# Last message layer and projections as one stage, with ScalarE evicting and biases added by products of ones

## The reference, cut to what matters

```
h = x
for _ in range(3):
    msgs = relu(h[src] @ W_edge + b_edge)
    agg  = segment_sum(msgs, dst, num_segments=50000)
    h    = relu(concatenate([agg, h], -1) @ W_agg + b_agg)
x1 = layernorm(x + h)                     # no gain, no bias, eps 1e-5
q, k, v, skip = (x1 @ W + b  for Wq, Wk, Wv, Wskip)
...                                       # attention over dst, feed-forward, two norms
```

## Time and profile before

| what | us |
|---|---|
| median of 3 runs | 6480.81 |
| lowest, highest | 6471.52, 6483.21 |
| the profiled execution | 6482.03 |
| its span | 6480.2 |
| PE busy | 4587.8 (71%) |
| DVE busy | 3774.3 (58%) |
| POOL busy | 3525.7 (54%) |
| ACT busy | 1885.8 (29%) |

### The profile page before, as it was taken

How to read it: one execution, slowest core, us unless ns; L and a number is a source line. 1 busy time by engine, 2 the same in 40 slices (tenths; PEclk the granted TensorE clock), 3 DMA queues, 4 the chain that set the end, 5 groups by cost and what they waited for, 6 DMA issues and landing times. The chain is left out here.

```text
span 6480.2 us, 105856 instructions
## 1 busy us (share of the span) xinstructions
PE 4587.8 (71%) x19910; PEld 2854.0 (44%) x19911; DVE 3774.3 (58%) x12450; ACT 1885.8 (29%) x4118; POOL 3525.7 (54%) x3741
## 2 busy tenths in 40 slices
PE   5666657777777777666666777466666666888887
PEld 3444445555555555444443333244444443333333
DVE  7666633333333333333347888577777776777777
ACT  0222223333333333011110000122222222666665
POOL 1555554444344443544434555666666653888887
PEclk9888878888878888777788999655555555999999
DMA  1333345545455454333336888433333332333333
GB/s 34 127 126 124 131 126 149 155 149 153 148 149 151 149 154 146 112 109 108 108 102 220 266 270 268 149 89 88 91 91 88 88 85 69 101 104 104 104 106 96
DMA packets 732213, 840.28 MB, mean 130 GB/s; under 512 B 150205, under 2 KB 575272, under 8 KB 732068
## 3 DMA queue, kind: packets, MB, share of 16 engines
q1 hardware_dynamic: 619172, 619.89, 29.9%
q0 software_dynamic: 112896, 218.94, 13.4%
HBM read 439.86 MB, written 398.61 MB: 129 GB/s over the span
## 5 line engine op out<-in xcount | busy, mean ns | idle before, releaser
L762 POOL DMA_INDIRECT mp_gathered<-msg_rows,other_idx x1176 | 1120.9, 953 | 1411.5 <-PE bank L781 902.1
L781 PE MATMUL bank<-mp_edge_hot,mp_gathered 128*128 128x256 bf16 x5292 | 933.6, 308 | 458.6 <-issue 400.7
L781 PEld LDWEIGHTS bank<-mp_edge_hot,mp_gathered 128*128 x5292 | 560.9, 106 | 743.6 <-issue 637.9
L840 ACT ACTIVATE mp_h_out<-bank,mp_b_agg 128x256 f32<-128x256 f32 x588 | 278.7, 474 | 1429.6 <-PE bank L799 749.3
L525 POOL DMA_INDIRECT by_window<-so_pay,so_pos_i x392 | 395.2, 1008 | 437.6 <-issue 305.5
L1206 POOL DMA_INDIRECT at_kv<-kv_rows,kv_idx x392 | 422.1, 1077 | 348.1 <-DVE at_v_e L1355 241.5
L874 DVE TENSOR_SCALAR mp_edge_hot<-digits,mp_first_col,column 128x256 bf16<-128x256 bf16 x1764 | 506.1, 349 | 109.6 <-issue 74.8
L799 PE MATMUL bank<-mp_h_in,mp_w_agg_h 128*128 128x256 f32 x1176 | 474.0, 491 | 109.1 <-issue 103.7
L897 DVE TENSOR_TENSOR mp_msg_out<-mp_rest,mp_msg_out 128x256 bf16<-128x256 f32 x392 | 166.3, 424 | 650.2 <-ACT mp_msg_out L853 393.2
L1490 POOL DMA_INDIRECT ff_agg<-at_rows,last_idx x392 | 414.1, 1056 | 96.7 <-issue 89.0
L1208 POOL DMA_INDIRECT at_q<-q_rows,node_idx x392 | 393.5, 1004 | 126.7 <-issue 126.7
(11 more groups left out here) (217 smaller groups left out, 9283.4 us busy)
## 6 DMA issues: line engine op xcount, KB each, us to landing
mp_h_in<-h_cols SPq DMA_DIRECT2D x588, 128.0 KB
h_cols<-mp_h_out SPq DMA_DIRECT2D x588, 128.0 KB
msg_rows<-mp_msg_out SPq DMA_DIRECT2D x392, 192.0 KB
kv_rows<-pn_proj SPq DMA_DIRECT2D x98, 512.0 KB
msg_rows<-so_msg_out SPq DMA_DIRECT2D x98, 384.0 KB
h_cols<-so_h_out SPq DMA_DIRECT2D x98, 256.0 KB
pn_h_in<-h_cols SPq DMA_DIRECT2D x98, 256.0 KB
x_rows<-pn_x_b SPq DMA_DIRECT2D x98, 256.0 KB
```

The source lines that it names most:

```text
L762: pool.indirect_dma_start(gathered[:, r * PARTS * D:(r + 1) * PARTS * D], None, core.msg_rows[layer % 2], bass.IndirectOffsetOnAxis(ap=cor ...
L781: product = nc.tensor.matmul(agg_bank[k], gathered[:, bass.ds(at + d * D, D)], hot, start=(first and d == 0), stop=True, skip_group_check= ...
```

## The change

`message_passing` keeps two layers (`range(LAYERS - 1)`) and loses the target counting. `project_nodes` is gone. A new stage `last_layer` does the third layer and the projections; it stands before `last_edges`. Its parts:

- The edge sums come out node by feature: the 0/1 matrix is now the weight and the gathered part is moved, so a block takes 3 tiles x 2 halves x 3 parts = 18 products of 128 columns. The h part likewise: the block's `h` columns are the weight, W_agg the moved part, one product per half. A group's four halves share one bank, begun by one product of ones (3 rows) with the bias split in three bf16 parts. h is no longer stored in `h_cols`, nor loaded and transposed by groups.
- DVE takes relu and adds x in one instruction, takes the moments, and makes 1/deviation in five small steps from a square root that ACT gives, with a shift for ACT. POOL only gathers.
- ACT normalises (four instructions), copies the transposed columns, and evicts all four projection tiles with a plain copy.
- Each projection tile is begun by a product of ones with the split biases; the identity is added to Wskip once, so that the skip part contains x1. DVE adds b2.
- The loop is written out for 8 blocks, with lags of up to 8 blocks; 0/1 matrices have 8 buffers instead of 4, target matrices 4 instead of 2; x, y and x1 have four.

The core of the diff:

```diff
-def project_nodes(core, x, w, b):
+def bias_parts(core, dve, chain, at, src, rest, hi, mid, parts):
+    nc = core.nc
+    nc.vector.tensor_copy(hi, src).then_inc(chain, 1)
+    dve.wait_ge(chain, at + 1)
+    nc.vector.tensor_tensor(rest, src, hi, ALU.subtract).then_inc(chain, 1)
+    nc.vector.tensor_scalar(parts, hi, core.ident[0:PARTS, 0:1], None, ALU.mult).then_inc(chain, 1)
...
+    return at + 7
+def last_layer(core, W_agg, b_agg, x, w, b):
+    rows_bank, x1_bank, proj_bank = bank[2:4], bank[0], [bank[1], bank[4], bank[5], bank[7]]
...
+            def store(g):
+                k = g % 2
+                reached(sp, xb2_ok, g + 1)
+                sp.dma_start(rows(core.x1_rows, g), x1_b2[k][:, :, :]).then_inc(st_x1[k], 16)
+                reached(sp, by_act, T * (g + 1))
+                sp.dma_start(rows(core.kv_rows, g), proj[k][:, :, 0:2 * D]).then_inc(st[k], 16)
+                sp.dma_start(rows(core.q_rows, g), proj[k][:, :, 2 * D:3 * D]).then_inc(st[k], 16)
+                sp.dma_start(rows(core.skip_rows, g), proj[k][:, :, 3 * D:4 * D]).then_inc(st[k], 16)
...
+            for n in range(NW + 10):
+                if n + RING - 1 < NW:
+                    reached(sp, block_mm, n)
+                    load_h(n + RING - 1)
+                if n % 2 == 0 and n // 2 + Q - 1 < NG:
+                    reached(sp, y_ok, n // 2)
+                    load_x(n // 2 + Q - 1)
+                if n % 2 and 0 <= n // 2 - 4 < NG:
+                    store(n // 2 - 4)
...
+            def add_tile(r, i, hot):
+                at = (i & (TILES - 1)) * (PARTS * D)
+                for half in range(2):
+                    to = rows_bank[r // 2 % 2][:, (r % 2 * 2 + half) * P:(r % 2 * 2 + half + 1) * P]
+                    for d in range(PARTS):
+                        product = nc.tensor.matmul(to, hot(half), gathered[:, bass.ds(at + d * D, D)], start=False, stop=True, skip_group_check=True)
+                return product
...
+            def project(g, q, j):
+                pe.wait_ge(cols_ok, g + 1)
+                for t in range(T):
+                    reached(pe, by_act, T * (g - 1) + t + 1)
+                    nc.tensor.matmul(proj_bank[t][:, :], core.ones[0:PARTS, :], proj_parts[:, :], start=True, stop=True, skip_group_check=True)
+                    nc.tensor.matmul(proj_bank[t][:, :], x1_cols[q % 2][:, t * P:(t + 1) * P], weights[:, :], start=False, stop=True,
+                                     skip_group_check=True).then_inc(mm, 1)
+            def turn(do):                       # PE
+                do(0, sum_edges)
+                do(0, count_targets)
+                do(-6, group(turn_x1))
+                do(-8, group(project))
...
+            def evict(g, q, j):
+                reached(act, st[q % 2], 48 * (2 * j + q // 2))
+                for t in range(T):
+                    act.wait_ge(mm, T * g + t + 1)
+                    nc.scalar.activation(proj[q % 2][:, t, :], proj_bank[t][:, :], ACT.Copy).then_inc(by_act, 1)
+            def turn(do):                       # ACT
+                do(0, group(roots))
+                do(-4, group(x1_columns))
+                do(-2, group(normalize))
+                do(-6, group(evict))
...
+            def add_rows(g, q, j):
+                dve.wait_ge(block_mm, 2 * g + 2)
+                dve.wait_ge(x_ld[q], 16 * (j + 1))
...
+                nc.vector.scalar_tensor_tensor(out=y[q][:, :, :], in0=rows_bank[q % 2][:, :].rearrange("p (t f) -> p t f", t=T), scalar=0.0,
+                                               in1=x_in[q][:, :, :], op0=ALU.max, op1=ALU.add).then_inc(y_ok, 1)
+                dve.wait_ge(y_ok, g + 1)
+                norm_stats(nc, dve, stat_c, g, y[q], stats[q], moments[q]).then_inc(mom_ok, 1)
...
+            def turn(do):                       # DVE
+                do(-3, group(add_rows))
+                do(-6, group(deviations))
+                do(-8, group(add_b2))
+                do(0, hots)
+                do(0, target_hots)
```

More of the change, by code:

```diff
@@ L741, in _ @@
                 told = [0] * (TILES // TOLD)
-                for layer in range(LAYERS):
+                for layer in range(LAYERS - 1):
                     if layer:
@@ L833, in _ @@
                 act.wait_ge(wts, 5 * 16)
[L834 to L835 removed]
+                for layer in range(LAYERS - 1):
+                    wins, turns_done = layer * NW, layer * (NW // RING)
                     def close_block(n, r, j):
@@ new lines, in last_layer, with rows, blocks, straight @@
+        x1_t, cols_ok, mm, by_act = (core.sem("ll_" + n) for n in (
+            "x1_transposed", "x1_cols_ready", "product", "proj_by_scalar"))
+        def rows(t, g):
+            return t[g * GR:(g + 1) * GR, :].rearrange("(p k) f -> p k f", k=T)
+        def blocks(eng, turn):
+            def straight(n):
+                def do(lag, step):
+                    if 0 <= n + lag < NW:
+                        step(n + lag, (n + lag) % TURN, (n + lag) // TURN)
+                turn(do)
+            for n in range(2 * TURN):
+                straight(n)
+            with aligned(eng, 2, NW // TURN) as j:
+                for r in range(TURN):
+                    turn(lambda lag, step: step(TURN * j + r + lag, (r + lag) % TURN, j + (r + lag) // TURN))
+            for n in range(NW // TURN * TURN, NW + 2 * TURN):
+                straight(n)
@@ new lines, in group, with at_second_block, edge_tiles @@
+        def group(step):
+            def at_second_block(n, r, j):
+                if r % 2:
+                    step(Q * j + r // 2, r // 2, j)
+            return at_second_block
+        words = {}
+        def edge_tiles(eng, n, r):
+            if r == 0:
+                words[eng.engine] = nc.values_load_multi_w_load_instructions(
+                    core.spans[0:1, bass.ds(n, TURN)], engines=[eng.engine], min_val=0, max_val=512 * NT - 1,
+                    skip_runtime_bounds_check_because="both halves are masked and only address tables of their size")[1]
+            word = words[eng.engine][r]
+            return word & 511, word >> 9
@@ L963, in project_nodes, with further @@
+        def further(eng, n, first, last, more):
+            with eng.If(first + (ALWAYS - 1) < last):
+                before = eng.value_load(core.more_before[0:1, bass.ds(n, 1)], min_val=0, max_val=NT - 1)
+                with eng.Fori(first + (ALWAYS - 1), last) as i:
+                    more(i, (before + i - (first + (ALWAYS - 1))) & 511)
         block = s.enter_context(nc.Block())
-        def rows(t, g):
-            return t[bass.ds(g * GR, GR), :].rearrange("(p k) f -> p k f", k=T)
@@ L1029, in turn, with roots @@
             def turn(do):
-                do(2, turn_h)
-                do(0, turn_x1)
-                do(-1, project)
-            turns(pe, turn)
+                do(0, sum_edges)
+                do(0, count_targets)
+                do(-6, group(turn_x1))
+                do(-8, group(project))
+            blocks(pe, turn)
         @block.scalar
         def _(act):
-            def x1_columns(g, k, i):
+            act.wait_ge(zero_ok, 2)
+            def roots(g, q, j):
+                act.wait_ge(mom_ok, g + 1)
+                reached(act, rstd_ok, g - Q + 1)
+                nc.scalar.activation(root[q][:, :], moments[q][:, :, 1], ACT.Sqrt, bias=eps_col[:, 0:1], scale=0.25).then_inc(root_ok, 1)
@@ new lines, in hot, with hots, more @@
+            def hot(to, n, i):
+                return nc.vector.tensor_scalar(to, core.digits[:, :], first_col[:, bass.ds(n, 1)], core.column[:, bass.ds(i, 1)],
+                                               ALU.add, ALU.is_equal)
+            def hots(n, r, j):
+                def more(i, at):
+                    dve.wait_ge(tile_mm, at + n + 1)
+                    hot(more_hot[:, bass.ds((at & 1) * W, W)], n, i + 1).then_inc(more_hot_ok, 1)
+                first, final = edge_tiles(dve, n, r)
+                reached(dve, block_mm, n - HOTS + 1)
+                for c in range(ALWAYS):
+                    made = hot(edge_hot[r % HOTS][:, c, :], n, first + c)
+                made.then_inc(edge_hot_ok, 1)
+                further(dve, n, first, final, more)
@@ L1114, in attention @@
+            blocks(dve, turn)
+            dve.wait_ge(dst_mm, NW)
+            nc.vector.tensor_copy(core.dst_count[0:NG, :], count_bank).then_inc(tabs_ok, 1)
 def attention(core, edge_attr, We):
```

329 lines of the change are left out of this document (174 added, 155 removed).

## The result

The kernel after takes 6204.39 us, the median of 4 runs (6200.82 to 6207.68), beside 6482.01 (6471.52 to 6491.08) for the kernel before in 4 runs. The ratio is 0.9572, with an interval of 0.9556 to 0.9589: 277 us less, where 122 were forecast and 6230 was the low end of the range. The direction was right and the size wrong.

The account below looks back on a forecast made before the run. PE's stream plus about 7 us per burst of gathers bounds the old layer. Start 20, 49 cycles of 28.0 us (1372), ends 12 and 11 make 1415 against 1537: 122 less, so 6359 us, range 6230 to 6560.

Parts of the forecast that it names:

- Array time per group, 10.0 us: PE in the new stage: products of a group of two blocks sum to 9.7 us, taken as 10.0 with idling.
- The 128-column edge products: PE's edge sums in the new stage: 36 products a group at 0.082 us each, 2.95 us (2.0 to 4.0).
- The ones: PE's new products of ones times bias parts: five a group, each twice 0.11 us, 1.1 us in all.
- Issue, 2.5 to 3.5 us a block: PE's instruction issue in the new stage: 2.5 to 3.5 us a block, 5 to 7 a group; the array ends last.
- Start 20, end 12 and 11: Around the new stage: 20 us before it, 12 for the last group's chain and stores, 11 for last edges and barrier.
- The burst, 8.0 us: PE's loss in each of 49 bursts of gathers in the new stage: 8.0 us, ends 3.7 and 12.
- the second rival: At PE's edge sums, a burst costs more with the longer stream: 12 us each, 196 us more, 6555; chance 0.25.
- The first rival: On PE, the stop hides under queued projections: loss 3.7 us a burst, 211 us less, 6150; chance 0.10.
- Rivals on the other side: New stage slower: dearer bursts, 6555, 0.25; PE loop code fetched again, 6498, 0.08; serial DVE/ACT/PE wait, 6460 to 6550, 0.07.

Follow-up runs that it names:

- Experiment 2: Kernel after, with the addresses of a tile's gathered parts worked out anew for the second half: 6459.93 us, ratio 0.9966.
- Experiment 1: Kernel after, with the long float32 product of each projection tile left out (x1 W not computed): 6022.45 us, ratio 0.930.
- experiment 6: Kernel after, with POOL gathering in bursts of four instead of eight (CHUNK 4) in all layers: 5940.48 us, ratio 0.9167.
- experiments 13 and 15: Kernel after, with gathers in fours and the projection's float32 product left out, run twice on chips without the stop: 5423.50 and 5408.43 us.

## Why the prediction was wrong

Direction and place held, and so did most terms. The step that failed is the price of a burst, which was carried over from the old layers without the cover that the new stream gives.

- *Array time per group, 10.0 us:* 10.2 by the rhythm of the blocks. The 128-column edge products came at the low end: 18 of them take 1.18 us, the last of them 0.22, so 0.96/17 = 0.056 us each, not 0.082. The Trainium skill's 81 ns for such a pair (TensorE: Matmul & The Clock Gate, "Back-to-back issue gap") is not what this trace shows. The ones were dearer than twice 0.11: 0.3 to 0.5 each. The two errors cancel by luck.
- *Issue, 2.5 to 3.5 us a block:* 1.9 undisturbed, since the addresses of the first half are used again (1809 register instructions of the main kind for 3528 products) and the projection lets PE's queue run ahead. Experiment 2 shows what it costs if they aren't: 256 us.
- *Start 20, end 12 and 11:* the first block ended 26 us after the layer before, and from the last block to attention it took 43 instead of 23: four projections of 5.7 us stand behind the last block, which the sum left out. Some 26 us too little.
- *The burst, 8.0 us:* this is the step that failed: "the loss per burst was 7.0", carried over and raised by one, with no overlap between the stop and the queued projection. A burst cost 4.1, 49 x 3.9 = 191 us less. Experiment 1 shows what made the difference: without the long products a burst costs the new stage 10 us and the pauses double (254 against 112 us). So without cover a burst costs this stage more than it cost the old layers, which is the second rival's direction, and some 6 of the 10 us lie under the transposes and the projection, which take 8.3 less 1.9 = 6.4 us of PE. With the 26 us above and 0.4 us more array time in each of 49 cycles, the three misses make -145 of the -153 us between 1415 and 1262.
- *The first rival* was this mechanism, at 3.7 us a burst and a chance of 0.10. Its mechanism is shown. Its price came near 4.1 by luck: it took 8.0 less 4.3, where the runs have 10 less 6. The argument that kept its chance low, that in the first layers 0.86 us more array work a block hid nothing, was misread: the last layer has the counts in place of part of it, so by busy time the first layers carry only (633.4 - 568.4)/196 = 0.33 us more a block, and none of it is a row of long products like the projection's 5.5 us.
- *Rivals on the other side:* no register instruction of the edge products took over 0.9 us, and a burst cost less than before, not more, as long as the projection covered it. The instruction queue moved 0.92 MB in the whole run, 0.93 in the kernel before, so nothing was brought again at the loop's returns. No wait between ACT, DVE and PE showed: PE's idle time is issue.

What a stop costs PE is not what its absence is worth. In the old layers PE lost the seven us to the stop and not to POOL: in layer one PE's waits for POOL are 8.3 us and its idle time put down to issue is 188, while POOL waits for PE 296.6 us, in 40 waits.

```profile
PE bank L781 <- issue: 134.2, 180, 6.3
PE bank L781 <- POOLq L748: 8.3, 4, 3.9
POOL mp_gathered L762 <- PE bank L781: 296.6, 40, 9.9
```

But without the stop the first two layers gain only 4.1 us a cycle, since POOL's own pace of 13.1 comes next, above PE's 10.0. In the new stage PE needs 20.4 a cycle, POOL's pace is hidden, and the whole 4.1 that a burst costs is gained. If the old last layer gains what the first two do, which no trace shows, that is why the change is worth 278 us with and without the stop. POOL's pace could have been read from the kernel before: a gather every 1.25 us and the landing of the last make 13 us for four blocks. I had looked at POOL's waits for PE alone.

What stays open is what in a burst holds PE's issue: the kind of the gather or more than four microseconds of POOL's descriptors without a break, and why some chips don't show it. Open too is whether fours hide the stop in the new stage by their length or by the cover. In the first layers, which have no long products, fours cost no more with the stop than without: 786 and 795 us from the first block to the last (experiment 6), and 805 to 812 in experiments 13 and 15.

## What to carry to other kernels

A stall's price belongs to the stream in which it was measured: before carrying it to another, look at what will stand queued when it begins, since long work runs on through it. A cycle less the pace of one engine is what a stall costs that engine, not what its removal is worth: for that, work out the pace of each engine that takes part, its waits for its own transfers among them, and take only what stands above the slowest. Work that is taken from an engine beside a stall may have been its cover (98 us taken, 66 given back). Here it paid to shorten the stall first and take the work away then: 95 of 98 us arrived. Moving work to an engine that has room can still fail by its place in that engine's order: two of four tiles gave 95 us, four gave nothing.

## What the runs showed of the hardware

- While POOL issues gathers without a break, PE's issue is held from about 4 us into the burst until about 2 us behind the last one (experiment 1). Products with fixed addresses are held too (97 us of pauses), and DVE's issue as well (111 register instructions over 0.4 us in the new stage, none without the stop). Bursts of four, 5 us long, with gaps of 5 us hardly show it: over 0.4 us are 4 of PE's register instructions in the new stage where eights have 51, and 14 of DVE's.
- It seems to depend on the chip: on two others no register instruction of PE's edge products took over 51 ns, and the kernel before took 5464 us instead of 6480. A gain that rests on the stop isn't the same everywhere. Gathers in fours and told early, which gained 48 us a layer with the stop, took 805 to 812 us a layer there (13 and 15 above), against 642 with eights: a loss of some 165.
- A register instruction on PE costs about 0.15 us where nothing long is queued before it (15 more made a block 2.2 us longer), and next to nothing behind a long product (0.1 us for the 15).
- Pairs of weight load and 128-column bf16 product follow each other at 0.056 us at the full clock (18 in 1.18 us, the last of them 0.22).
